# Attention with two rings of PSUM banks: maxima of the next head group between exponentials of the current one

## What is computed

```python
q = _rope(q, ROPE_THETA); k = _rope(k, ROPE_THETA)
scores = jnp.einsum('bhqd,bhkd->bhqk', q, k) * D ** (-0.5)
scores = jnp.where(causal[None, None], scores, -jnp.inf)
weights = jax.nn.softmax(scores, axis=-1)
out = jnp.einsum('bhqk,bhkd->bhqd', weights, v)
```

## Time and profile before

| | us |
|---|---|
| device time, median of 3 runs (lowest, highest) | 1244.29 (1241.22, 1248.29) |
| span of the profiled execution | 1235.5 |
| PE busy, share of the span | 895.0 (72%) |
| DVE busy | 600.8 (49%) |
| ACT busy | 426.9 (35%) |

### The profile page before, as it was taken

The page is one execution under the profiler, slowest core; times in us unless marked ns, Lnnn a source line. Parts: engine busy times, 40 slices in busy tenths (PEclk is TensorE's granted clock), DMA queues, the critical chain, the costliest instruction groups (busy, mean ns, idle before and its releaser), DMA issues.

```text
span 1235.5 us, 16046 instructions
## 1 busy us (share of the span) xinstructions
PE 895.0 (72%) x5604; PEld 448.6 (36%) x5604; DVE 600.8 (49%) x1338; ACT 426.9 (35%) x546; POOL 77.7 (6%) x51
## 2 busy tenths in 40 slices
PE   4377788797876967868865522947886968879786
PEld 3134576243333333433433222612333433333333
DVE  4573202663553734735172545495643725537442
ACT  1243332144424344435612400013434334344354
POOL 1710002000000000000007200000000000000000
PEclk9679998577978789889976755855978869689899
DMA  6110001001001010010022200000000010010001
GB/s 248 66 37 1 1 1 45 33 1 40 12 29 39 0 39 20 19 39 1 4 92 77 76 26 0 1 0 1 6 35 35 6 39 12 27 39 0 39 1 34
DMA packets 19563, 37.62 MB, mean 30 GB/s; under 512 B 2880, under 2 KB 12864, under 8 KB 19008
## 3 DMA queue, kind: packets, MB, share of 16 engines
q1 hardware_dynamic: 19264, 36.79, 8.2%
q10 hardware_dynamic: 256, 0.26, 0.1%
HBM read 29.44 MB, written 7.34 MB: 30 GB/s over the span
## 4 chain that ended last, share of the span: by engine, by line
PE 46%; DVE 16%; issue 16%; DMA 8%; POOL 5%; ACT 4%; SPq 4%; DVEq 0%; ACTq 0%; POOLq 0%
PE ps L939 42%; DVE maxes L882 8%; DMA R<-k_thirds 7%; SPq L435 3%; PE ps L1181 2%; SPq L437 2%; POOL rope L485 2%; POOL rope L488 1%; ACT R L633 1%; POOL third L492 1%; ACT R L628 1%; PE ps L1158 1%; DVE bnst L668 1%; ACT third L553 1%; ACT third L555 1%
## 5 line engine op out<-in xcount | busy, mean ns | idle before, releaser
L939 PE MATMUL ps<-R 128*128 128x128 f32 (+10 forms) x2240 | 568.5, 364 | 166.0 <-DMA R<-k_thirds 74.8
L882 DVE TENSOR_REDUCE maxes<-ps 128x1 f32<-128x512 f32 (+3 forms) x640 | 385.6, 635 | 321.9 <-PE ps L939 310.7
L628 ACT ACTIVATE R<-ps 128x1024 f32<-128x1024 f32 (+1 forms) x320 | 292.6, 937 | 409.8 <-PE ps L939 405.2
L939 PEld LDWEIGHTS ps<-R 74*128 74x128 bf16 (+4 forms) x2240 | 237.2, 133 | 468.6 <-issue 171.7
L939 PE MATMUL ps<-R,vgrp 128*32 128x512 f32 (+3 forms) x1536 | 176.9, 532 | 0.0
L939 PE MATMUL ps<-maskq,identb 128*128 128x128 bf16 x512 | 122.6, 257 | 0.0
L939 PE MATMUL ps<-maskk,identb 128*128 128x128 bf16 x512 | 121.8, 238 | 0.0
L939 PEld LDWEIGHTS ps<-maskk,identb 128*128 128x128 bf16 x512 | 55.0, 107 | 26.1 <-issue 16.4
L939 PEld LDWEIGHTS ps<-maskq,identb 128*128 128x128 bf16 x512 | 58.6, 114 | 5.2 <-issue 4.4
L939 PE MATMUL ps<-count,R 128*128 128x1 f32 x64 | 18.3, 357 | 54.7 <-DVE R L823 52.1
L510 POOL COPY vgrp<-vals 128x288 f32 (+1 forms) x16 | 7.1, 453 | 793.1 <-PE ps L939 793.0
(11 more groups left out here) (147 smaller groups left out, 539.0 us busy)
## 6 DMA issues: line engine op xcount, KB each, us to landing
R<-q_thirds SPq DMA_DIRECT2D x96, 96.0 KB
R<-k_thirds SPq DMA_DIRECT2D x96, 96.0 KB
R<-in_w SPq DMA_DIRECT2D x2, 2048.0 KB, 11.6
q_thirds<-third SPq DMA_DIRECT2D x8, 384.0 KB, 2.6
k_thirds<-third SPq DMA_DIRECT2D x8, 384.0 KB, 3.3
rot<-in_rot SPq DMA_DIRECT2D x1, 1024.0 KB, 5.2
R<-in_spread SPq DMA_DIRECT2D x1, 1024.0 KB, 5.7
out<-x SPq DMA_DIRECT2D x4, 256.0 KB, 2.3
```

Of the source, the lines that this page charges most:

```text
L628: act.activation(probs[SLOT[step]][:, h, 0:w], flat[:, 1024 * (n % 2):1024 * (n % 2) + w], ACT.Exp, scale=SCALE).then_inc(s.exp, 1)
L882: dve.tensor_reduce(dst, src, AX.X, ALU.max).then_inc(s.max_read, 1)
L939: return pe.matmul(out_, lhsT, rhs, start=first, stop=last)
```

## The change

The two-pass scheme stays, but nearly all of its parts are new.

- **Max pass.** Each head has its own 32 rows (`MR = 4 * D`: only two of the three thirds of q and k, 4 terms) in new tiles `qmx` and `kmx`, which lie in `rope`. A unit is two heads at once in a pair of banks, 512 columns for each head: 18 units a group (9 patterns for two pairs of heads), two pairs of banks in turn (banks 0 to 3). The two heads' matmuls are issued alternately and sit on different rows of the array. In the two diagonal patterns the mask goes in first, as one 512-column matmul for each bank (lhsT `identb`, rhs `maskq` broadcast four times). DVE reduces 2 x 512 columns in one instruction.
- **Exp pass.** 36 units of one bank and 512 columns (`UNITS`), in a ring of three banks (4 to 6) that the shift's transpose and the output's transposes also use ("cells"). The mask is 128 columns as before. `probs` is a ring of 18 units.
- **Values.** The same products by half of the queries (`STEP`, 10 steps), summed in bank 7. ACT copies the sums (`outT`) and also the transposed output (`raw`); DVE divides once for each batch entry (`normalise_heads`).
- **Shift.** One transpose a group; the two DMAs are now issued by SP, and read 32 partitions of `shiftT`.
- **Loads.** For each group 16 DMAs of 16 partitions x 1024 for the max operands (q: outermost dimension 2, broadcast; k: outermost dimension 2, the two thirds) and 6 DMAs of 24 partitions x 4096 for the exp operands (outermost dimension 3 as before, twice as long each). The same bytes of exp operands as before, and 512 KB more.
- **Order.** `attention_order` sorts all units of all eight groups by a planned time (`MAX_US`, `EXP_US`, `SHIFT_LAG_US`, `LEAD_US`), written out without a loop. A group has 23.2 us in that plan, and its exp pass follows its last max unit by about 8.4 us.

```diff
+MAX_US, EXP_US, TOP_US, SHIFT_LAG_US, LEAD_US = 1.25, 0.56, 0.7, 3.0, 3.5
+PV_LAG, OUT_LAG = 5, 3
...
+            def load_for_max(L, g):
+                r = g % 2
+                for h in range(HG):
+                    head = slice(g * HG * D + h, (g + 1) * HG * D, HG)
+                    rows_h = slice(MR * h, MR * h + MR)
+                    for n in range(2):
+                        rows_n = slice(MR * h + 16 * n, MR * h + 16 * n + 16)
+                        sp.dma_start(qmx[rows_n, r, :],
+                                     q_dram[L][n:n + 1, head, :].to_broadcast([2, D, T])).then_inc(s_mload[r], 16)
+                        sp.dma_start(kmx[rows_n, r, :], k_dram[L][0:2, head, :]).then_inc(s_mload[r], 16)
...
+                for i in range(3):
+                    rows_i = slice(3 * D * i, 3 * D * i + 3 * D)
+                    sp.dma_start(qop[rows_i, r, :, :].rearrange("p h t -> p (h t)"),
+                                 q_rows[i:i + 1].to_broadcast([3, D, HG * T])).then_inc(s_xload[r], 16)
+                    sp.dma_start(kop[rows_i, r, :, :].rearrange("p h t -> p (h t)"), k_rows).then_inc(s_xload[r], 16)
...
+            def attention(L):
+                cells = L * CELLS
+                for what, g, *arg in ORDER:
+                    n = L * NG + g
+                    if what == "shift":
+                        cells += 1
+                        sp.wait_ge(s_cells_read, cells)
+                        for part in range(2):
+                            sp.dma_start(qop[KR + part:KR + part + 1, g % 2, :, :],
+                                         shiftT[HG * TB * part:HG * TB * part + HG * TB, :]
+                                         ).then_inc(s_shift_in[g % 2], 16)
+                    elif what == "exp" or what == "out":
+                        cells += 1
+                        if arg[0] == NU - 1 and g + 2 < NG:
+                            sp.wait_ge(s_cells_full, cells)
+                            load_for_exp(L, g + 2)
+                    elif what == "max" and arg[0] == NM - 1 and g + 2 < NG:
+                        sp.wait_ge(s_rows_full, (n + 1) * NM)
+                        load_for_max(L, g + 2)
...
+                        if diagonal:
+                            for k in range(2):
+                                mm(bank(pair + k).rearrange("p (n c) -> p n c", n=4), identb[:, :], maskq[:, :].unsqueeze(1).to_broadcast([P, 4, P]), True, False)
+                        c = 0
+                        for i, k0, w in pieces:
+                            for k, h in enumerate(heads):
+                                rows_h = slice(MR * h, MR * h + MR)
+                                last = mm(bank(pair + k)[:, c:c + w], qmx[rows_h, r, P * i:P * i + P],
+                                          kmx[rows_h, r, k0:k0 + w], not diagonal, not diagonal or c + w == BANK)
+                            c += w
+                        last.then_inc(s_rows_full, 1)
...
+                    elif what == "exp":
+                        if arg[0] == 0:
+                            pe.wait_ge(s_xload[r], (L * NG // 2 + g // 2 + 1) * 6 * 16)
+                            pe.wait_ge(s_shift_in[r], (L * NG // 2 + g // 2 + 1) * 2 * 16)
+                        if cells >= 3:
+                            pe.wait_ge(s_cells_read, cells - 2)
```

More of the change, by code:

```diff
@@ L86 @@
[L86 to L96, removed]
-        else:
[L98 to L135, removed]
-    return order
@@ L139 @@
[L139 to L158, removed]
+UNITS, STEP = [], []
@@ new lines @@
+for half in range(2):
+    first = 4 * half
+    for j in range(4 * half):
+        STEP.append((len(UNITS), 4, half, [j]))
+        UNITS += [[(j, h, BANK * half, BANK, 0)] for h in range(HG)]
+    q = BANK * half
+    STEP.append((len(UNITS), 4, half, [first]))
+    UNITS += [[(first, h, q, 512, 0)] for h in range(HG)]
+    STEP.append((len(UNITS), 4, half, [first + 1, first + 3]))
+    UNITS += [[(first + 1, h, q + 128, 384, 0), (first + 3, h, q + 384, 128, 384)] for h in range(HG)]
+    STEP.append((len(UNITS), 2, half, [first + 2]))
+    UNITS += [[(first + 2, h, q + 256, 256, 0), (first + 2, h + 1, q + 256, 256, 256)] for h in (0, 2)]
@@ new lines, with place @@
+NU = len(UNITS)
+RING = NU // 2
+NS = len(STEP)
+HALF_END = [max(n for n in range(NS) if STEP[n][2] == half) for half in range(2)]
+PATTERN = [[(i, 0, 512)] for i in (4, 5, 6, 7)] + [
+    [(2, 0, 256), (3, 0, 256)], [(6, 512, 256), (7, 512, 256)],
+    [(1, 0, 128), (3, 256, 128), (5, 512, 128), (7, 768, 128)],
+    [(i, P * i, 128) for i in range(4)], [(i, P * i, 128) for i in range(4, 8)]]
+NM = 2 * len(PATTERN)
+def place(step, head, j):
+    first, count = STEP[step][0], STEP[step][1]
+    for u in range(first, first + count):
+        for piece in UNITS[u]:
+            if piece[0] == j and piece[1] == head:
+                return u, piece
@@ new lines, with cell_of, shift_cells, summed_steps @@
+ORDER = attention_order()
+CELL_KINDS = ("exp", "shift", "out")
+CELLS = sum(what[0] in CELL_KINDS for what in ORDER)
+CELL_AT = {}
+for what in ORDER:
+    if what[0] in CELL_KINDS:
+        CELL_AT[what] = len(CELL_AT)
+def cell_of(n, unit):
+    return n // NG * CELLS + CELL_AT[("exp", n % NG, unit)]
+def shift_cells(n):
+    return n // NG * CELLS + CELL_AT[("shift", n % NG)] + 1
+def summed_steps(unit):
+    n, u = divmod(unit, NU)
+    return n * NS + next(k for k in range(NS) if u < STEP[k][0] + STEP[k][1]) + 1
@@ L388, in block_kernel @@
         s1.own = sem("routed_own")
+        s_ones = sem("kop_ones")
+        s_floor = sem("maxes_floor")
+        s_mload = [sem(f"max_operands{r}") for r in range(2)]
+        s_xload = [sem(f"exp_operands{r}") for r in range(2)]
+        s_shift_in = [sem(f"shift_in{r}") for r in range(2)]
+        s_vgrp = sem("group_values")
+        s_rows_full = sem("rows_full")
+        s_rows_read = sem("rows_read")
+        s_cells_full = sem("cells_full")
+        s_cells_read = sem("cells_read")
+        s_top = sem("shift_ready")
+        s_pv = sem("values_summed")
+        s_outT = sem("sums_copied")
         s_const = sem("constants")
```

445 lines of the change are left out of this document (222 added, 223 removed).

## The result

The changed kernel takes **1304.7 us** (median of 4 runs, 1301.3 to 1308.6). The kernel before took 1242.8 us beside it (median of 4, 1239.4 to 1248.3). The ratio is 1.051, with a 95% interval of 1.046 to 1.056: the change makes the kernel 5% slower. The prediction said 1324, slower.

What follows compares the result with a forecast made beforehand. SP's queue was taken to bound each turn, the shift waiting behind 22 loads: 30 + 29 = 59 us against 50.6. Change 40.4 - 1 + 36.5 + 3.5 = 79 on span 1235.5, plus 8.8, gave 1324 us; range 1185 to 1395.

Steps and rivals of the forecast that it cites:

- From the last max unit to the first exp unit (30 us): In each turn, the shift waits behind SP's 22 loads, issues and transfers: 30 us, bounds 28 to 32.
- From there to the next last max unit (29 us): TensorE's work from first exp unit to next last max unit: 23.8 us plus 5 for low clock, said 29.
- The low clock behind the wait: After each turn's wait TensorE resumes at clock 0.50 for 10 us, which costs 5 us.
- the 1.6 us that I added for 48 small matmuls in the max units: In TensorE's max units, 48 small matmuls cost at least 0.06 us each, adding 1.6 us.
- that rival: Max units' matmul pairs on TensorE don't overlap: 12 x 2.6 us more, total 1355; chance included in the main mechanism's 0.70.
- The period (59 us): One group's turn: 30 us to the first exp unit plus 29 to the next last max unit, against 50.6 before.
- A layer (408 us): From a layer's first exp unit to its end: first stretch, five turns of 59, group 6 and last passes, together 408 us.
- The whole group at full clock (31.7 us of TensorE): All TensorE work of one group at clock 1.00: 31.7 us, the period if nothing else held it.
- Span and median: Whole program: span 1235.5 + 79 = 1315 us, with 8.8 between span and median 1324.
- an L470 that lands 2 to 3 us after its issue: Sign against the forecast: the shift's DMA on SP's queue lands 2 to 3 us after issue, then turns of 48 us.
- Two other signs: Signs for the forecast: turns of 59 us, and the clock at 0.50 for about 10 us after each first exp unit.
- The rival "all is hidden": Loads are issued and done within TensorE's 7.9 us, period 31.7, total near 1008 us; chance 0.05.

Runs made afterwards that it cites:

- e2_exp_loads_behind: The changed kernel with the six exp loads issued behind the shift's two DMAs, the 16 max loads still ahead, all on SP's queue; 1133.8 us.
- e10_act_lead_even: The changed kernel with the shift's DMAs on ACT's queue, the plan's lead 7.5 us instead of 3.5, an exp unit priced 0.64 instead of 0.56; 1002.4 us.
- e4_wide: The changed kernel with thirds laid out in DRAM by group, so a load's outermost dimension is 16 or 24; issue order kept; 1194.3 us, 0.963 of before.
- e6_busy_wait: The changed kernel with 84 additional 512-column matmuls on TensorE ahead of the wait for the shift, in groups 1 to 5 of each layer; 1430.0 us.

## Why the prediction was right

The direction, the mechanism and its place were right: a turn waits some 20 us at its first exp unit for a shift that stands behind 22 loads. By the steps of the prediction:

- **From the last max unit to the first exp unit (30 us).** Measured 29.3 (269.9 to 299.2). Issues came quicker than assumed, 0.64 apart for the 16 max loads (10.35 instead of 11.9), and the exp loads ran at the share of 0.19 that the earlier trace rows had. e2_exp_loads_behind shows both parts. The Trainium skill, "DMA: Bandwidth & Descriptors", section "Queues, rings and completion order", says that each engine consumes a queue's descriptors in order; e2_exp_loads_behind agrees, by 9.8 us of transfers that stood ahead of the shift. The 2 engines of a max load, on which no row of before bore, agree with the share of 0.11 in the window of the max loads alone:

```profile
270.00:279.50 9.50, 8.18 (x67) 2.96 (x65) 7.03 (x9) 5.16 (x10) 0.00 (x0) 1.00 0.11 35
```

- **From there to the next last max unit (29 us).** Measured 25.0 (299.2 to 324.15), 4 less. Two terms were mis-sized. The low clock behind the wait lasted 6 us and not 10, which costs 3 instead of 5. And the 1.6 us that I added for 48 small matmuls in the max units do not exist: eight of 128 columns, in row-wise pairs, take no longer than two of 512. So the pairs overlap, and that rival falls. Start to start it is 0.33 for the small ones, the same as for two of 512 columns in row-wise pairs:

```profile
323.72 0.40 PE L987 MATMUL ps<-rope 32*128 32x128 bf16 x8
324.05 0.39 PE L987 MATMUL ps<-R 74*128 74x512 bf16 x1
```

- **The period (59 us).** Measured 54.4, by these two terms.
- **A layer (408 us).** Measured 400.4 in the first (240.5 to 640.9). Five turns gave 23 us less than forecast. Against that stand terms that were too small, 15 us together. The first stretch took 29.4 and not 27, at a clock of 0.60. Group 6's first exp unit came 25 us behind its last max unit and not 23.5. From there to the last max unit it took 34 and not 29, since the clock stayed at 0.50 for 41 us (554 to 595), 28 of them behind the wait and not 10; and from there to the last exp pass 9 and not 7. The last pass took 31 and not 26.5, with outputs of all groups divided at its end. The second layer took 400.6 (884.9 to 1285.5); one of its turns took 63.9 us, with the clock at 0.50 for 27 us behind the wait, a case that the sum left out. The errors have opposite signs, so the total was closer than its parts by luck.
- **The whole group at full clock (31.7 us of TensorE).** No turn of the changed kernel runs at full clock throughout. One of e10_act_lead_even does, and takes 31.82 us, but TensorE is busy in only 30.23 of 31.80 there; the rest is waits. So the term was some 1.5 us too large, which fits the 1.6 us for small matmuls that do not exist, and that the turn equals it is chance:

```profile
322.50:354.30 31.80, 30.23 (x274) 11.75 (x275) 22.17 (x21) 20.88 (x41) 0.45 (x1) 1.00 0.15 56
```

- **Span and median.** Of the 19 us by which 1324 is too high, 13 are the span (1315 against 1302). The other 6 come from the 8.8 us that I added "between span and median". Every run has its device time 2 us above its own span (1304.23 above 1302.1). So what lies around the program is 2 us, and the other 6.8 are presumably the distance between the profiled execution of before and a middle one: spans of before in the later comparison went from 1230 to 1248. That difference belonged in the range and not in the sum.

The prediction had named an L470 that lands 2 to 3 us after its issue as a sign against itself. The profile's median of 2.3 us looks like just that, but the longest of the 32 is 14.9, and the median was no sign: TensorE's wait is 12 us longer, so the landing that the profile infers is too early. The wait at TensorE and e2_exp_loads_behind decided. Two other signs came out smaller than named: turns of 54 and not 59 us, and in the turns shown 6 and not 10 us at 0.50 behind the wait. The rival "all is hidden" (1008 us) expected the plan in the code to hold once the queue was no matter. It did not: with the shift out from behind the loads that plan took 1092 and 1067 us. The 1002 us needed the longer lead and the even plan as well.

## What to carry to other kernels

A DMA that an engine waits for goes ahead of prefetches, or onto another queue. Being short does not help it: it pays for the issues and for the transfers of all that stand before it, here 14.7 us to its issue and 14.5 from there, of which some 10 are the loads' transfers, for 16 KB. When a plan is a table of prices, look at what else each queue does between two steps of it; the plan that brought 90 us on one queue (1092 to 1002) cost 207 on the other (1067 to 1273). And once the long wait is gone, look for short rows of units bound by another engine: here the clock fell behind five of six such rows, with a wait of 1.3 us in each.

## What the hardware showed that I had not expected

- The granted clock fell from 1.00 to 0.50 behind a row of max units in which TensorE was busy 2.10 of 3.48 us, although it was never idle longer than 1.3 us. The first such row of the layer brought no fall. With the rows spread out, it stayed at 1.00 for 225 us of the profiled execution.
- How long the clock stays down under dense work differs from turn to turn. In the changed kernel it was mostly back at 1.00 some 6 us behind the wait, but took 28 us in one turn of the first layer and 27 in one of the second; in e4_wide it took 14 or 34 us in a turn, and 35 us of 512-column matmuls without a gap ran at 0.52 in e6_busy_wait. This is open.
- The issue of a load whose outermost dimension is 16 or 24 took SP mostly 0.31 to 0.42 us, against 0.60 to 0.70 for the same bytes with an outermost dimension of 2 or 3.
- A DMA's landing in the profile can be some 12 us early (a median of 2.3 us for the shift, whose exp unit started 14.5 us behind its issue). Read it from the start of the engine that waits.
